# Depthwise convolution of a linear-attention block: from 120 full-array matmuls against banded matrices to 240 matmuls of 32x32 tiles

## The reference, cut to what matters

```
qkv = einsum('bchw,oc->bohw', ln(x), w_qkv)              # 192 channels: 24 groups of 8
dw  = depthwise 5x5 convolution of qkv, padding 2, w_dw
pw  = einsum('bgihw,goi->bgohw', dw in 24 groups, w_pw)  # 8 -> 8 within each group
ms  = concat(qkv, pw)                                    # 16 heads of 8: q, k, v each
q, k = relu(q), relu(k);  kv = k.T @ [v, 1];  att = (q @ kv)[:-1] / (q @ kv)[-1]
x   = x + batchnorm(w_proj @ att)
t   = tokens of x;  t = t + sum over the top 2 of 8 experts of w_e * (gelu(ln(t) @ W1[e] + b1) @ W2[e] + b2)
```

## Time and profile before

| | before |
|---|---|
| median of 3 runs | 126.23 us (126.22 to 126.4) |
| the profiled execution's own time | 125.97 us |
| its span, first to last instruction | 124.3 us |
| granted TensorE clock, mean | 0.998 |
| PE busy | 119.4 us (96%) |
| DVE / ACT / POOL busy | 88.6 / 84.9 / 29.4 us |

### The profile page before, as it was taken

The page is one execution under the profiler, slowest core; times in us unless marked ns, Lnnn a source line. Parts: engine busy times, 40 slices in busy tenths (PEclk is TensorE's granted clock), DMA queues, the critical chain, the costliest instruction groups (busy, mean ns, idle before and its releaser), DMA issues.

```text
span 124.3 us, 2671 instructions
## 1 busy us (share of the span) xinstructions
PE 119.4 (96%) x918; PEld 94.9 (76%) x918; DVE 88.6 (71%) x279; ACT 84.9 (68%) x197; POOL 29.4 (24%) x34
## 2 busy tenths in 40 slices
PE   6998999999999999999999999999999999999991
PEld 5397899999999889896786786666766767666660
DVE  0689999999987887998896039994607236077972
ACT  4479999999972948259797499194690947919300
POOL 7308999900000000303370005000000000000370
PEclk9999999999999999999999999999999999999999
DMA  3779400000000000000000038961069891001001
GB/s 101 217 176 228 136 3 0 3 5 0 0 0 0 5 0 0 0 5 0 0 0 3 7 69 233 235 148 45 11 167 221 228 235 41 5 3 42 0 0 42
DMA packets 5590, 8.11 MB, mean 65 GB/s; under 512 B 1442, under 2 KB 4042, under 8 KB 5578
## 3 DMA queue, kind: packets, MB, share of 16 engines
q1 hardware_dynamic: 5344, 7.80, 25.2%
q10 hardware_dynamic: 234, 0.15, 0.4%
HBM read 7.36 MB, written 0.59 MB: 64 GB/s over the span
## 4 chain that ended last, share of the span: by engine, by line
PE 80%; DVE 7%; ACT 4%; DMA 3%; issue 2%; POOL 1%; POOLq 1%; SPq 0%; DVEq 0%
PE PS L975 53%; PE PS L1204 17%; PE PS L1091 3%; DMA X<-in_x_dram 3%; DVE BAND L870 2%; DVE STATS L610 2%; PE PS L1097 2%; ACT MS L433 1%; PE PS L1128 1%; POOL XP L416 1%; PE PS L1114 1%; PE PS L1159 1%; PE PS L1051 1%; DVE XP L906 1%; DVE WY L896 1%
## 5 line engine op out<-in xcount | busy, mean ns | idle before, releaser
L538 ACT ACTIVATE MS<-PS,B 128x512 f32<-128x512 f32 x48 | 29.1, 689 | 7.2 <-PE PS L975 6.9
L975 PE MATMUL PS<-QP,BAND 128*128 128x120 f32 (+2 forms) x240 | 27.0, 275 | 0.2 <-DVE QP L666 0.2
L975 PEld LDWEIGHTS PS<-QP,BAND 128*128 128x128 f32 x240 | 26.9, 192 | 0.4 <-issue 0.4
L975 PE MATMUL PS<-XS,W1H 128*128 128x512 f32 x64 | 26.5, 414 | 0.0
L975 PE MATMUL PS<-XS,W1L 128*128 128x512 f32 x64 | 25.3, 395 | 0.0
L1204 PE MATMUL PS<-MS,W 128*64 128x256 f32 x192 | 22.3, 383 | 0.0
L846 DVE SCALAR_TENSOR_TENSOR WY<-PS,B,BAND 128x256 f32<-128x256 f32 x24 | 10.5, 480 | 15.2 <-PE PS L1204 14.5
L1204 PEld LDWEIGHTS PS<-MS,W 128*64 128x64 f32 x192 | 13.2, 137 | 8.5 <-ACT MS L538 1.5
L456 ACT ACTIVATE BAND<-RS,PW 128x80 f32<-128x80 f32 x64 | 17.3, 447 | 0.0
L975 PEld LDWEIGHTS PS<-XS,W1H 128*128 128x128 f32 x64 | 12.0, 188 | 4.8 <-issue 0.9
L975 PEld LDWEIGHTS PS<-XS,W1L 128*128 128x128 f32 x64 | 12.1, 189 | 1.8
(11 more groups left out here) (128 smaller groups left out, 168.2 us busy)
## 6 DMA issues: line engine op xcount, KB each, us to landing
BAND<-spread_dram SPq DMA_DIRECT2D x14, 256.0 KB, 4.8
W<-in_w_dram SPq DMA_DIRECT2D x3, 512.0 KB, 6.4
X<-in_x_dram SPq DMA_DIRECT2D x2, 256.0 KB, 3.7
BAND<-spread_dram SPq DMA_DIRECT2D x4, 128.0 KB, 3.2
out_dram<-XP SPq DMA_DIRECT2D x4, 128.0 KB, 1.7
W<-spread_dram SPq DMA_DIRECT2D x2, 256.0 KB, 5.7
VEC<-in_vectors_dram SPq DMA_DIRECT2D x1, 132.0 KB, 3.0
SELF<-in_select_dram ACTq DMA_DIRECT2D x1, 100.8 KB
```

The source lines that it names most:

```text
L538: act.activation(hidden(n), PS[:, h_bank(n), :], ACT.Gelu, bias=B1[:, k:k + 1]).then_inc(gelu_done, 1)
L975: return pe.matmul(PS[0:parts, bank, cols[0]:cols[1]], lhsT, rhs, start=start, stop=stop)
```

## The change

The band matrices go. The convolution works on blocks of four image columns by 8 channels, that is 32 partitions, and four heads lie side by side on the 128 partitions (rows 32r to 32r+31 are head 4g+r). An output block of four columns takes two input blocks (`after` 0 and 1, shifted by two columns), so for each group and kernel row there are two 32x32 weight matrices, all cut from one strip `BANDS` of 8 shifts.

- `rs()` is 32 matmuls with 40x32 weights over 30 columns (float32, so 64 records) into one bank in place of four steps of 4; ACT copies it in one operation, which stands before the square root on ACT. The casts of its inputs (L428, L615, L616) go, and their DMAs carry less. Six full-array warm-up matmuls follow `rs()`, and four stand ahead of the convolution.
- The scaled projection goes to `MSQ`. PE turns it over (`turn_heads`, 24 transposes of 128x128); ACT and DVE place each result, 128x512, into `QP` (`place_own`, then `place_before`, six each).
- POOL builds all six parts of `BANDS` (320 elements a partition each) and copies the first heads' q into `MS` (eight copies).
- The convolution is 240 matmuls of 32x32 weights: `conv_q` 5 rounds of 16 (4 row strips by 4 column strips), `conv_vk` 10 rounds of 16. A round has 512, 480 or 448 columns.
- Results are copied to `CV` (`take_conv`, two of 128x512 on DVE and two on ACT for each part) and turned back on PE: the queries by 16 matmuls against `SUM` (`turn_back_q`, inside `conv_vk` after its fourth round, with the eight transposes of the input, `turn_input`), k and v by 16 transposes at the end (`turn_back`). DVE and ACT then make the second heads' `VM` and `KR` from PSUM (`second_heads`, three operations a pair).
- The W1 split, the batch-norm arithmetic and the residual stand in the convolution on DVE; the centred residual stands between `read_kv(0)` and `read_kv(1)`.

The diff, cut to its core (indentation shortened):

```diff
         STATS_BANKS, WQC_BANK, WARM_BANK = (0, 1, 6, 2), 7, 7
-        WARM_UPS, TILE_BANKS = 3, (7, 5)
-        RS_BANKS = (3, 4, 5, 7)
-        XT_BANKS = (3, 4)
+        WARM_UPS, WARM_UPS_BEFORE_QKV, WARM_UPS_BEFORE_CONV, TILE_BANKS = 3, 6, 4, (7, 5)
+        RS_BANK = 3
+        XT_BANKS = (5, 7)
         QKV_BANKS = (0, 1), (2, 6), (3, 4), (5, 7)
-        SCALED_V, SCALED_S = 8, 8
-        ON_POOL = 2
-        CONV_RING = (5, 6, 7, 0)
-        LAST_BANKS = (1, 0, 2)
+        KINDS = (0, 2, 1)
+        TURNED_BANKS = (0, 1), (2, 6), (3, 4)
+        CONV_BANKS = (5, 7, 0, 1), (6, 2, 3, 4)
+        BACK_BANKS, BACK_Q_BANKS = (0, 7, 5, 1), (0, 1)
...
         pool.wait_ge(x_in[k], 16)
         pool.tensor_copy(*in_token_order(k, 2 - k, 3 - k)).then_inc(xp_p, 1)
+    pool.memset(QP[:, :, :, :, 4, :].rearrange("p q g s t -> p (q g s) t"), 0.0).then_inc(zeros_set, 1)
     pool.wait_ge(cst_in, 16)
     pool.tensor_copy(VM[:, :, :, :, :, HH].rearrange("p s h r b -> p (s h r) b"),
                      PAR.unsqueeze(1).broadcast_to([128, 8 * PAIRS, 2])).then_inc(ones_set, 1)
-    pool.wait_ge(rs_copied, 4)
     pool.wait_ge(pw_in, 16)
-    for g in range(ON_POOL):
-        pool.tensor_tensor(*band_factors(g), ALU.mult).then_inc(band_p, 1)
+    pool.wait_ge(ones_set, 1)
+    for r in range(4):
+        rows = slice(32 * r, 32 * r + 32)
+        pool.tensor_copy(PWQ[rows, :, :, :], PW[rows].rearrange("p (g r q) o -> p r q g o", g=2, r=4)[:, r])\
+            .then_inc(pwq_made, 1)
+    pool.wait_ge(pwq_made, 4)
+    pool.wait_ge(rs_copied, 1)
+    pool.wait_ge(r1_ready, 1)
+    for n in range(3):
+        for g in range(2):
+            pool.tensor_tensor(*band_factors(KINDS[n], g), ALU.mult).then_inc(band_p, 1)
     pool.wait_ge(vec_in, 16)
     pool.tensor_scalar(INV[:, 0, :], VEC[:, 3 * C:4 * C], BN_EPS, None, ALU.add).then_inc(bn_guarded, 1)
@@ -389,6 +420,13 @@
     pool.tensor_tensor(INV[:, 1, C // 2:C], INV[:, 0, C // 2:C], HALF[:, C // 2:C], ALU.pow).then_inc(inv_ready, 1)
+    pool.wait_ge(scaled_v, 8)
+    pool.wait_ge(scaled_s, 8)
+    for s in range(PAIRS):
+        for x in (0, 2):
+            pool.tensor_copy(MS[:, 4 * s + x:4 * s + x + 2, 0:HH].rearrange("p x (h i) -> p x h i", h=8),
+                             first_half(s, 0)[:, 2 - x:4 - x]).then_inc(q_first, 1)
...
-    def copy_rs(k):
-        act.wait_ge(rs_ready, k + 1)
-        act.activation(*quarter_rs(k), ACT.Copy).then_inc(rs_copied, 1)
+    def copy_rs():
+        act.wait_ge(rs_ready, 1)
+        act.activation(RS[:, :, :].rearrange("p x d -> p (x d)"), PS[:, RS_BANK, 0:SHIFTS * 2 * 3 * DY], ACT.Copy)\
+            .then_inc(rs_copied, 1)
     act.wait_ge(wqc_ready, 1)
     act.activation(WQC[:, :], PS[:, WQC_BANK, 0:QKV], ACT.Copy).then_inc(wqc_copied, 1)
-    copy_rs(0)
...
-    def bands(g):
-        for o in range(I):
-            i = act.activation(band[:, g].rearrange("p d (x o) -> p o (d x)", o=I)[:, o],
-                               RS[:, g].rearrange("p d x -> p (d x)"), ACT.Copy, scale=PW[:, g, o:o + 1])
-        i.then_inc(band_s, 1)
+    def place_own(n, g):
+        act.wait_ge(heads_turned, 2 * n + g + 1)
+        act.activation(blocks(n, g, 0), head_columns(n, g), ACT.Copy, scale=CST[:, C_OWN:C_OWN + 1]).then_inc(qp_s, 1)
+    def take_conv(n):
+        for r in (2, 3):
+            act.wait_ge(conv_ready, 4 * n + r + 1)
+            act.activation(CV[:, n, r, :], PS[:, CONV_BANKS[n][r], :], ACT.Copy).then_inc(cv_s, 1)
...
+    def first_k(s):
+        act.activation(KR[:, s, :, 0:HH].rearrange("p x (h i) -> p x h i", h=8), first_half(s, 1), ACT.Relu)\
+            .then_inc(k_first, 1)
+    def second_heads(s):
+        act.wait_ge(back_turned, s + 1)
         for b in range(2):
-            to, of, one = masked_v(s, 0, b)
-            act.activation(to, of, ACT.Copy, scale=one)
-    act.wait_ge(rs_copied, 4)
-    act.wait_ge(pw_in, 16)
-    bands(2)
-    bands(5)
-    bands(8)
-    act.wait_ge(scaled_v, SCALED_V)
-    act.wait_ge(scaled_s, SCALED_S)
+            act.activation(VM[:, s, 1, :, b, 0:HH], second_half(s, 0), ACT.Copy, scale=PAR[:, b:b + 1])
+        act.activation(KR[:, s, :, HH:HD], second_half(s, 1), ACT.Relu).then_inc(second_by_s, 1)
     act.wait_ge(cst_in, 16)
...
-            for b in range(2):
-                to, of, one = masked_v(s, 1, b)
-                act.activation(to, of, ACT.Copy, scale=one).then_inc(v_more, 1)
-    second_heads(0)
-    second_heads(1)
+    def second_q(s):
+        act.wait_ge(q_turned, s % 2 + 1)
+        act.activation(MS[:, 4 * s:4 * s + 4, HH:HD], second_of_q(s), ACT.Copy).then_inc(q_s, 1)
+    second_q(0)
+    second_q(2)
+    take_conv(1)
     second_heads(2)
+    second_heads(3)
...
+    def place_before(n, g):
+        dve.wait_ge(qp_s, 2 * n + g + 1)
+        dve.wait_ge(zeros_set, 1)
+        dve.scalar_tensor_tensor(out=blocks(n, g, 1), in0=head_columns(n, g), scalar=CST[:, C_BEFORE:C_BEFORE + 1],
+                                 in1=blocks(n, g, 1), op0=ALU.mult, op1=ALU.add).then_inc(qp_v, 1)
+    def take_conv(n):
+        for r in (0, 1):
+            dve.wait_ge(conv_ready, 4 * n + r + 1)
+            dve.tensor_copy(CV[:, n, r, :], PS[:, CONV_BANKS[n][r], :]).then_inc(cv_v, 1)
+    def split_low(part):
+        cols = slice(E * HID // 2 * part, E * HID // 2 * (part + 1))
+        dve.tensor_tensor(W1L[:, cols], W1[:, cols], W1H[:, cols].bitcast(F32), ALU.subtract).then_inc(w_low, 1)
...
+    def second_heads(s):
+        dve.wait_ge(back_turned, s + 1)
+        for b in range(2):
+            dve.tensor_scalar(VM[:, s, 1, :, b, 0:HH], second_half(s, 0), PAR[:, b:b + 1], None, ALU.mult)
+        dve.tensor_scalar(KR[:, s, :, HH:HD], second_half(s, 1), 0.0, None, ALU.max).then_inc(second_by_v, 1)
+    def second_q(s):
+        dve.wait_ge(q_turned, s % 2 + 1)
+        dve.tensor_copy(MS[:, 4 * s:4 * s + 4, HH:HD], second_of_q(s)).then_inc(q_v, 1)
...
+    dve.wait_ge(cst_in, 16)
+    for n in range(3):
+        place_before(n, 0)
+        place_before(n, 1)
+    dve.wait_ge(scaled_s, 8)
+    for s in range(PAIRS):
+        first_v(s)
+    take_conv(0)
+    dve.wait_ge(w_high, 2)
+    split_low(0)
+    split_low(1)
+    dve.tensor_tensor(WGS[:, 1, :], WG[:, :], WGS[:, 0, :].bitcast(F32), ALU.subtract).then_inc(w_low, 1)
...
-    move_last(0)
+    second_q(1)
+    second_q(3)
+    normalisation()
+    residual()
+    take_conv(1)
+    second_heads(0)
+    second_heads(1)
     read_kv(0)
-    split_low(1)
-    dve.tensor_tensor(WGS[:, 1, :], WG[:, :], WGS[:, 0, :].bitcast(F32), ALU.subtract).then_inc(w_low, 1)
+    centred_residual()
...
-    def rs(k):
-        pe.wait_ge(sel_high, 1)
-        pe.wait_ge(wd_split, 1)
-        for j in range(4):
-            xo = 4 * k + j
-            i = mm(RS_BANKS[k], (120 * j, 120 * j + 120), SEL[:, (W - 1 - xo) * I:(W - 1 - xo) * I + 128],
-                   WD[:, :], True, True)
+    def rs():
+        pe.wait_ge(sel_in, 16)
+        pe.wait_ge(dw_in, 16)
+        for n in range(SHIFTS):
+            for r in range(4):
+                at = 2 * 3 * DY * n
+                i = pe.matmul(PS[32 * r:32 * r + 32, RS_BANK, at:at + 2 * 3 * DY].rearrange("p (g d) -> p g d", g=2),
+                              SEL[:, I * (SHIFTS - 1 - n):I * (SHIFTS - 1 - n) + BLOCK * I],
+                              WD[:, :].rearrange("k (g r d) -> k r g d", g=2, r=4)[:, r], start=True, stop=True)
         i.then_inc(rs_ready, 1)
     def qkv(jp):
@@ -1029,62 +1050,118 @@
     pe.wait_ge(ident_made, 1)
     turn_tokens(0)
-    warm_up(1)
+    warm_up(1, WARM_BANK)
     turn_tokens(1)
     centre_weights()
-    rs(0)
-    rs(1)
-    rs(2)
+    rs()
+    warm_up(WARM_UPS_BEFORE_QKV, TILE_BANKS[1])
     pe.wait_ge(wqc_copied, 1)
-    rs(3)
...
-                       QP[:, 3 * h + q, B * (first + dy - PAD):B * (last + dy - PAD)], dy == PAD, dy == DY - 1)
-            if q == 2 or h == 7:
-                i.then_inc(conv_ready, 1)
+    def turn_heads(n, pairs, last):
+        for g in range(2):
+            for s in pairs:
+                i = pe.transpose(PS[:, TURNED_BANKS[n][g], 128 * s:128 * s + 128],
+                                 MSQ[:, s, KINDS[n], 4 * g:4 * g + 4].rearrange("p h x i -> p (h x i)"), IDT[:, :])
+            if last:
+                i.then_inc(heads_turned, 1)
+    def turn_back():
+        pe.wait_ge(cv_v, 4)
+        pe.wait_ge(cv_s, 4)
+        pe.wait_ge(xb_ready, 2)
+        pe.wait_ge(q_v, 2)
+        pe.wait_ge(q_s, 2)
+        for s in range(PAIRS):
+            for r in range(4):
+                i = pe.transpose(PS[:, BACK_BANKS[s], :].rearrange("p (x k r o) -> p r k x o", x=4, k=4, r=4)[:, r],
+                                 CV[:, 1, r, 128 * s:128 * s + 128], IDT[:, :])
+            i.then_inc(back_turned, 1)
+    def turn_back_q():
+        pe.wait_ge(cv_v, 2)
+        pe.wait_ge(cv_s, 2)
+        pe.wait_ge(sum_made, 1)
+        for k in range(2):
+            for half in range(2):
+                s = 2 * half + k
```

(61 more changed lines are left out.)

283 lines of the change are left out of this document (110 added, 173 removed).

## The result

The changed kernel takes 125.17 us (median; 124.9 to 125.21) beside 126.16 us for the kernel before on the same chip: a ratio of 0.992, interval 0.9899 to 0.9942. Forecast were 123.4 us and a gain of 2.8 us; the gain is 1.0. Run again at the end of the study, on another occasion, it took 125.8 us, ratio 0.9964 [0.9942, 0.9985]: faster in both, by less than 1%. One run of it at 233.69 us and one of the kernel before at 137.36 us were disturbed and are left out. The profiled execution has a span of 123.4 us (before: 124.3).

What follows compares the result with a forecast made beforehand. PE's convolution, 27.03 us ahead of attention, was taken as the bound. Convolution -14.5, later start +2.85, work inside +4.8, its end to `attend(0)` +4.1: 2.8 us earlier, 123.4 us; 8 in 10 range 121.0 to 128.0.

Steps and rivals of the forecast that it cites:

- Up to the convolution: PE's work before the convolution: its start moves from 13.15 to 16.0 us, +2.85.
- `rs` rival: Before the convolution: `rs()` at 0.055 us a record ends 1.9 us later, total 125.3 us; chance 0.08.
- The price of a tile round: Convolution on PE: 16 tiles abreast take 0.83 us a round, 15 rounds 12.5 us in place of 27.0.
- rounds partly abreast: Convolution rounds: issue gaps or short inner runs bring a round to 0.95 to 1.2 us, total 125.2 to 129; chance 0.10.
- Inside the convolution: Between convolution rounds on PE: `turn_back_q`, `turn_input` and switches add 4.8 us.
- From the end of the convolution to `attend(0)`: Copies, transposes, then DVE's list up to `attend(0)`: 8.5 us in place of 4.4, none of it covered.
- E: The end of the convolution on PE, rounds and drain included, forecast at 33.3 us.
- From there to the end: From `attend(0)` to the kernel's end: distance unchanged at 79.7 us.
- The rival on the other side: Convolution: tiles not abreast at full clock, a round takes 1.67 to 1.76 us, total 136 to 137; chance 0.14.
- The clock rival: PE's clock falls to 1.2 GHz in gaps after or transposes before the convolution: 124.4 to 126.4 us; chance 0.12.

## Why the prediction was right or wrong

The direction was right, 125.17 lies inside the range, and the mechanism, a long convolution cut short by sixteen tiles abreast, is what happened. The size was wrong: 1.0 us gained, not 2.8. By its own steps, `attend(0)` came at 43.73, not 41.8; the 1.93 us are

- *Up to the convolution*: 16.0 forecast, 15.24 measured, -0.76. `rs()` took 0.75 us (1.6 taken, bounds 0.5 and 3.5); the warm-ups and the transposes were as costed to 0.25 us, and without its warm-ups the kernel starts the convolution at the same time. The `rs` rival did not occur.
- *The price of a tile round*: **the step that failed.** 0.83 us taken for 474 columns, 0.985 measured, so 15 rounds 14.8 and not 12.5: +2.3. Of this the 1.93 us hold 2.08, 1.59 in the first nine rounds and 0.49 in the last six; the other 0.2 I had already added by rounding the stretches up. The passes were costed rightly, and even a little high (0.80 us for two of 480 columns). The missing term is some 0.2 us at most rounds' turn, 0.19 on average. I had it as a rival, "rounds partly abreast", 0.95 to 1.2 us, with a chance of 0.10; it named gaps between rounds, which is what it was, and gave it 125.2 to 129, of which 125.17 is the lower edge; I held it for the less likely one. Nothing in the trace of before shows a stream as dense as this. The row that I leaned on, the start's warm-up, is one round of eight tiles, 32 records with the loads; it can show neither the turn to the next round nor a full window, as the kernel with eight tiles confirms (0.80 us for a round of 480 columns).
- *Inside the convolution*: 4.6 us forecast from `turn_back_q` to the next round, 4.59 measured.
- *From the end of the convolution to `attend(0)`*: 8.5 forecast, 9.12 measured, +0.62. DVE's list behind the copies was costed within 0.1 us (7.2 where I had 7.1), and a wait of 0.18 for `num(0)` comes on top; the copies came 0.34 later (1.74 with the wait, not 1.4), since ACT's strips end 0.56 us behind DVE's. The path through PE and ACT I had at E + 7.7; it ended at E + 9.0, for `qt` could start only at E + 5.9 behind `kv`, and `relu_qt(0)` behind it. I called it "not last"; it is level with DVE's list, and the kernels that shorten one or the other, or both, show it.
- *From there to the end*: 79.7 forecast, 79.67 measured. The clock stayed full, and moved work on DVE, ACT and POOL stayed covered, as forecast.

That 125.17 lies as near to 123.4 as it does is luck in part: the start came 0.76 us early, since `rs()` was costed too high, and this makes up for some of the 2.7 us lost behind it.

The rival on the other side, tiles not abreast at the full clock, fell: 18 records at a time, and rounds equal in any order. The clock rival did not occur, but my argument against it was misread: in the stretch from 44.57 to 55.19 PE is busy for all of the 10.62 us, so it shows nothing about waits. What shows it is the kernel without warm-ups, and the gaps of 1.18 and 0.78 us in the changed kernel.

The limit of this account: that the loss comes from a cap of about 64 records in flight is inferred, not seen; it is borne out by three kernels, one run each (half the tiles: none; half the columns: the same; half the records for a matmul: none), and by the count, but two rounds on each side of the turning back nearly escape it, and that stays open. So do the two stalls of the half-column kernel.

## What to carry to other kernels

When a stage behind the change was said to hang on one engine's list, work out the other path with the same care, since a list shortened alone gains nothing where two are level (1.6 us for both edits together, 0.1 and nothing for each). And work moved "inside" a busy stretch covers nothing there: the best place for the way back was behind the convolution, where PE stood idle for 1.18 us until the copies were there.

## What was not expected of the hardware

- A stream of float32 32x32 tiles loses some 0.2 us at most turns of a round of sixteen, and none with eight tiles; with bfloat16 at most 0.015.
- Passes on different tiles start 7 ns apart in the first round of a stream and mostly 16.7 ns apart in later ones; with bfloat16 some 3.5 and 8.3 ns.
- `conv_q` in short rounds stops twice for 0.43 and 0.80 us with nothing in the profile that holds PE.
- Once up, PE's clock fell to 1.2 GHz in the bfloat16 kernel only (0.58 granted on average between 22 and 30 us). Ahead of it PE had waited 1.31 and 2.10 us for DVE, with 1.1 us of short passes between them. Gaps of 1.18 and 0.78 us among longer work, in the changed kernel, left it at 2.4.
- When the clock rises at the start differs between executions of one kernel, and moves everything behind it by about 1 us.
